# Last stage of a fused attention and expert kernel: the load queue begins a tile's rows ahead of its weight copies

## What is computed

```python
def _L1_ffn_ref(hidden_states, norm_weight, router_w, sw1, sb1, sw2, sb2, ew1, eb1, ew2, eb2):
    normed = hidden_states * rsqrt(mean(square(hidden_states)) + 1e-08) * norm_weight
    shared = jnp.maximum(normed @ sw1 + sb1, 0.0) @ sw2 + sb2
    flat = normed.reshape(-1, d)                       # 4096 tokens x 128
    probs = jax.nn.sigmoid(flat @ router_w.T)          # 8 experts
    scores, idx = jax.lax.top_k(probs, 2)
    w = scores / (jnp.sum(scores, axis=-1, keepdims=True) + 1e-06)
    comb = comb.at[jnp.arange(T)[:, None], idx].add(w)
    h = jnp.maximum(jnp.einsum('td,edh->teh', flat, ew1) + eb1, 0.0)   # hidden 512
    eo = jnp.einsum('teh,eho->teo', h, ew2) + eb2
    return shared + jnp.einsum('teo,te->to', eo, comb)
```

## Time and profile before

| What | us |
|---|---|
| median of three timed runs | 1502.99 (1501.4 to 1507.45) |
| the profiled execution's own time | 1501.84 |
| its span in the trace | 1500.0 |
| what lies around the span | 1.84 |

### The profile page before, as it was taken

How to read it: one execution, slowest core, us unless ns; L and a number is a source line. 1 busy time by engine, 2 the same in 40 slices (tenths; PEclk the granted TensorE clock), 3 DMA queues, 4 the chain that set the end, 5 groups by cost and what they waited for, 6 DMA issues and landing times. The chain is left out here.

```text
span 1500.0 us, 35809 instructions
## 1 busy us (share of the span) xinstructions
PE 1261.6 (84%) x13441; PEld 1047.8 (70%) x13441; DVE 1012.2 (67%) x2018; ACT 890.2 (59%) x1661; POOL 599.2 (40%) x650
## 2 busy tenths in 40 slices
PE   4999998399999999994899999999972576699880
PEld 3777776277877787783798889888962564587760
DVE  5888887576777677764356676767665865576662
ACT  3888887566666666653455566566642455486750
POOL 3222222155555555564223332424121575165561
PEclk9999999599999999997899999999995688799995
DMA  4222221333221332132100000000001221146646
GB/s 140 92 91 93 94 99 50 120 86 92 76 64 45 92 79 69 42 89 75 48 13 17 9 16 9 17 10 9 3 2 42 83 78 35 47 138 222 209 132 181
DMA packets 88083, 109.04 MB, mean 73 GB/s; under 512 B 13290, under 2 KB 54890, under 8 KB 87914
## 3 DMA queue, kind: packets, MB, share of 16 engines
q1 hardware_dynamic: 82922, 96.46, 20.9%
q0 software_dynamic: 4992, 10.30, 2.1%
HBM read 61.11 MB, written 29.82 MB: 61 GB/s over the span
## 5 line engine op out<-in xcount | busy, mean ns | idle before, releaser
L818 POOL TENSOR_TENSOR b_h_lo<-b_h,b_h_hi 128x512 fp32r<-128x512 f32 x168 | 216.6, 1294 | 179.7 <-ACT b_h_hi L842 179.3
L837 ACT ACTIVATE b_zg<-b_zg 128x512 f32<-128x512 f32 x168 | 97.7, 582 | 82.5 <-PE b_zg L882 82.3
L842 ACT ACTIVATE b_h_hi<-b_h 128x512 fp32r<-128x512 f32 x168 | 105.3, 627 | 64.9 <-DVE b_h L1047 64.9
L1047 DVE TENSOR_TENSOR b_h<-b_zg,b_uw 128x512 f32<-128x512 f32 x168 | 116.2, 692 | 32.1 <-ACT b_zg L837 26.8
L1919 POOL DMA_INDIRECT planes_dram<-d_y_out,d_back x92 | 94.2, 1024 | 95.3 <-DVE d_y_out L2227 68.9
L2196 DVE TENSOR_TENSOR d_h_lo<-d_h,d_h_hi 128x512 fp32r<-128x512 f32 x124 | 85.1, 690 | 66.6 <-ACT d_h_hi L1957 32.3
L1040 DVE TENSOR_TENSOR b_uw<-b_zu,b_gw 128x512 f32<-128x512 f32 x128 | 88.2, 689 | 58.0 <-PE b_zu L882 51.3
L1586 DVE TENSOR_TENSOR c_oT_lo<-c_oy,c_oT_hi 128x512 fp32r<-128x512 f32 x64 | 44.1, 689 | 93.7 <-ACT c_oT_hi L1329 93.7
L1246 POOL TENSOR_TENSOR c_prob<-c_prob,c_recip 128x512 f32<-128x512 f32 x64 | 65.5, 1045 | 99.5 <-DVE c_recip L1579 99.5
L318 POOL TENSOR_TENSOR a_qx<-a_qT,headmask 128x256 f32<-128x256 f32 x64 | 37.9, 614 | 150.5 <-ACT a_qT L353 150.5
L525 DVE TENSOR_REDUCE a_top<-a_score_ps 128x8 f32<-128x1024 f32 x64 | 78.1, 1220 | 18.7 <-PE a_score_ps L416 18.7
(11 more groups left out here) (352 smaller groups left out, 4135.4 us busy)
## 6 DMA issues: line engine op xcount, KB each, us to landing
rows_dram<-a_blank SPq DMA_DIRECT2D x32, 520.0 KB, 3.2
b_gw<-gates_dram SPq DMA_DIRECT2D x64, 256.0 KB, 3.7
d_up_slot<-d_up_tab SPq DMA_DIRECT2D x15, 512.0 KB
d_down_slot<-d_down_tab SPq DMA_DIRECT2D x15, 512.0 KB
d_xg<-rows_dram SPq DMA_DIRECT2D x23, 260.0 KB
b_gm<-gates_dram SPq DMA_DIRECT2D x32, 160.0 KB, 3.8
c_craw<-in_c_ctxT_dram SPq DMA_DIRECT2D x16, 256.0 KB, 3.0
d_pay<-planes_dram SPq DMA_DIRECT2D x16, 256.0 KB, 4.6
```

The lines of the kernel that those rows point to most:

```text
L818: pool.tensor_tensor(h_lo[:, m % HS, :], h[:, m % HF, :], h_hi[:, m % HS, :].bitcast(F32), ALU.subtract).then_inc(lo_done.sem, 1)
L837: act.activation(zg_ps[:, n % ZG, :], zg_ps[:, n % ZG, :], ACT.Silu).then_inc(sg_done.sem, 1)
L842: act.activation(h_hi[:, m % HS, :], h[:, m % HF, :], ACT.Copy).then_inc(hi_done.sem, 1)
L1047: dve.tensor_tensor(h[:, n % HF, :], zg_ps[:, n % ZG, :], uw[:, n % 2, :], ALU.mult).then_inc(h_done.sem, 1)
```

## The change

In the turn of step k the block that gathers the rows of job k+2 is moved from behind the up and down weight copies to ahead of them. For the first planned tile the rows now also wait for the plan (`planned`), since the wait that covered them stood in the weight block. Nothing is computed otherwise; number, size and queue of all transfers stay.

```diff
@@ -1839,6 +1839,22 @@
                 weights.sync(sp, *share(k, c))
                 if c:
                     return
+                if FIRST <= k + 2 < JOBS:
+
+                    t = k + 2 - FIRST
+                    if t == 0:
+                        wait_scattered(sp, GROUPS)
+                    sp.wait_ge(xT_done.sem, xT_done.at(k + 1))
+                    sp.wait_ge(tail_done.sem, tail_done.at(t - 1))
+                    if t < E:
+                        block_rows = rows[t * REGION:t * REGION + TILE, :]
+                    else:
+                        if t == E:
+                            sp.wait_ge(planned, 2)
+                        r = sp.value_load(tile_row[0:1, t - E:t - E + 1], min_val=0, max_val=E * REGION)
+                        block_rows = rows[bass.ds(r, TILE), :]
+                    sp.dma_start(xg[:, t % 2, :, :], block_rows.rearrange("(u p) f -> p u f", p=P)
+                                 ).then_inc(xg_in[t % 2], 16)
                 if MOVED <= k + 2 < JOBS:
 
                     i, slot = k + 2 - MOVED, (k + 2 - MOVED) % WS
@@ -1859,20 +1875,6 @@
                     sp.wait_ge(y_done.sem, y_done.at(k + 1 - WS + 1))
                     sp.dma_start(down_slot[:, slot, :].bitcast(F32), down_tab[:, bass.ds(e, 1), :].rearrange("p a f -> p (a f)").bitcast(F32)
                                  ).then_inc(down_in[slot], 16)
-                if FIRST <= k + 2 < JOBS:
-
-                    t = k + 2 - FIRST
-                    ...
-                    sp.dma_start(xg[:, t % 2, :, :], block_rows.rearrange("(u p) f -> p u f", p=P)
-                                 ).then_inc(xg_in[t % 2], 16)
 
             ticks(step)
```

## The result

Over 20 runs of each kernel on the same chip, the kernel after took a median of 1501.27 us (1494.04 to 1508.83) and the kernel before 1506.86 us (1499.38 to 1516.66). The ratio is **0.996, 95% interval 0.9944 to 0.9977**: the change saves 0.4%, some 6 us, where 10.2 were forecast. The profiled execution of the kernel after took 1502.43 us, its span 1500.6 us, and that is not less than the span of the profiled execution before, 1500.0 us. So the trace of after shows an execution in which nothing was won, and its question is what took the gain back.

The account below looks back on a forecast made before the run. The prediction took TensorE's 6.48 us a tile as the floor and late rows as most of the 12.8 us lost above it. Less 2.65 us that stay, 10.2 us were to go, giving 1492.8 us, range 1488.5 to 1501.5.

Parts of the forecast that it names:

- What bounds it: Planned tiles: TensorE's own work is the floor at 6.48 us a tile; 12.8 us are lost between tiles 5 and 19.
- Rows moved ahead: SyncE's queue: rows go out 4.2 to 5.8 us sooner, after the tail, and the `d_t` waits for `xg` go whole.
- Copies moved behind, at no cost: Bias, up and down go out behind the rows, bias 0.4 to 1.6 us later; 4.6 us of cover, cost nothing.
- SP's turn: SyncE's turn of loads and issues takes 5.83 us, 0.65 under the new pace; at worst 6.23.
- The rival in which SyncE sets the pace: SyncE's turn of 7.2 us leaves no gain, 1503 us (0.12, with anything unseen); longer turns make it slower, about 1510 (0.06).
- The new wait for the plan: First planned tile's rows: the added wait is on one semaphore long reached and costs nothing.
- What stays: ScalarE's late waits for `z` of TensorE, cause unknown, go on costing TensorE two gaps, 2.65 us.
- The sum: 12.8 - 2.65 = 10.2 us gained over the planned tiles, for a median of 1492.8 us.
- ScalarE's late results set the pace: Rival: late results every second tile keep 9.7 of the 12.8 us; gain 3.1, 1499.9 us; chance 0.20.

Follow-up runs that it names:

- before again: The kernel before, unchanged, run against itself in a comparison where it took about 1484 us: 1482.72 against 1483.78 us, ratio 0.9999.
- before, static: The kernel before, old order, with rows' places and experts from constants, against the kernel before: 1482.8 against 1484.2 us (0.999), 1491.04 against 1500.16 us (0.9936).
- after, third time: The kernel after, unchanged, against the kernel before in a comparison where that took 1483.78 us: 1481.0 us, ratio 0.9982.
- type S: The comparisons in which the kernel before took 1500 to 1507 us; in two others it took 1484 us.
- early loads: The kernel after with all 30 register loads made before the planned tiles' copies, against the kernel before: ratios 0.9975 twice (before near 1484 us), 0.9936 and 0.994 (1500.16, 1504.31).

## Why the prediction was right in direction and wrong in size

**What bounds it: right.** The pace of 6.48 us a tile is TensorE's own and the floor. Kernels with nothing else in the way took 123.06 to 123.08 us for 19 tiles; the prediction had 123.16.

**Rows moved ahead: right.** They were to go out 1.2 to 2.4 us after the tail. In after a tail's last step ends at 1362.22 + 0.16 = 1362.38 and the rows go out at 1364.10, 1.7 us later. The waits of `d_t` for the DMA of `xg` are gone, in every profile of the new order.

```profile
1362.22 0.16 DVE L2240 SCALAR_TENSOR_TENSOR d_back<-d_pad,d_tail 128x4 int32<-128x4 f32 x1
```

**Copies moved behind, at no cost: right.** No view of after names a wait for `up_slot` or `down_slot`, not even where SyncE's turn took 6.49 us from rows to down: the 4.6 us of cover held. From the rows' issue to the bias an undisturbed turn needs 0.89 us (1409.87 to 1410.76); the prediction took 1.48.

**SP's turn: right**, for undisturbed turns. 1409.87 to 1416.42 is 6.55 us, the pace of the tiles, and TensorE never waits for it. One reading in it was wrong: that no turn of before without a wait exceeds 6.2 us. From the rows at 1394.27 to those at 1400.86 are 6.59 us, and `y_sb` (1395.13) and the tail that SyncE asked for (1394.12) had long ended; it is one of the turns with slow steps. The rival in which SyncE sets the pace is out: TensorE's waits name neither slot's DMA, and tiles come at 6.48 us wherever there is no hold.

**The new wait for the plan: right**, nothing of it is seen.

**What stays: the step that failed.** The prediction gave 2.65 us to ScalarE's late results and the other 10.2 of the 12.8 us to the late rows. It is the other way about. The late rows by themselves cost 3.3 us (before again), 3.1 and 2.1 us (before, static). The remaining 9.6 us or more of before came with the holds and were absent where there were none; what stayed in after was 14.4, 7.3 and 7.0 us, not 2.65. That most of it was disguised in before is argued from the traces and not shown by itself: the holds of before stand beside slow steps of SyncE, up to 0.70 us for a register step that took 0.18 at most in before again, and behind slow steps what came last was the rows. Even in the table only 6.6 us of TensorE's waits named the rows; the other 3.6 of the 10.2, the restarts too short to be listed, were given to them without a reason. The table of waits put the time down to `xg`, since it names the last comer, and the prediction read that as the cause. In the earlier trace rows ScalarE's waits for `z` have 21.2 us. Some 10 us of that is ordinary and costs nothing (after, third time, has 10.0 in 16 waits of up to 0.6 us and loses none), but the rest is in long waits, and the earlier trace rows showed two of them behind matmuls that had long finished; the prediction wrote that down, said that it couldn't tell the cause, and priced only the two gaps of TensorE that they ended last.

It also took for granted that what stays stays as it was. On type S the one profile of before has four holds of 2.46 to 4.54 us, the three of after have one or two of 4.8 to 6.7 us. One of those outlasts the slack between jobs, leaves TensorE idle for 4.4 to 4.8 us at a stretch, and brings down the granted clock, which the small gaps never did (0.97 to 0.96 in place of 1.00). Why they differ in shape was not shown.

**The sum.** The medians of type S gained 5.6 us in the first comparison and 3.1 and 3.5 in the two later ones. The loss was 12.9 us in one profile of before, and 14.4, 7.3 and 7.0 in three of after, 9.6 in the mean: 3.3 less. That agrees, though with one profile of before it could hardly fail to be near. Between one and two holds an execution lie 7 us, so a single pair of profiles could not have shown a gain of this size, and the pair above showed none. The low end of the range has a slip of 0.1 us: 1490.2 less 1.6 is 1488.6.

**The rivals.** The first, "ScalarE's late results set the pace", was the nearest in its mechanism and its time (1499.9 forecast, 1501.27 measured), though it expected one gap of 1.39 us in every second tile and not one or two long ones. Its gain of 3.1 us is what the two later comparisons gave. Its support, that such waits come in the stretch with copies and not before, holds against 1300 to 1332 us only: around 1240 us they were longer. At 0.20 its chance was too low: the wait with the largest sum at ScalarE had no explanation, and an unexplained wait ought to have held more of the chance than the 2.65 us gave it. The measured time lies within the range, 0.2 us from its upper end. That says little: the range was built on a median of 1502.99 us from three executions, and the twenty of the comparison have 1506.86. By the bound of 0.5% the result is no change.

## What to carry to other kernels

A wait's releaser is the one that came last, not the cause: before the sum of such a line is taken as what a change wins, look whether the engine named, and the queue that feeds it, are themselves slow in those turns and quick in others; if they are, find out by what. A wait for an engine whose records show it as long finished is time of its own and doesn't go when the next best cause is removed; price it with all that is long beyond the ordinary wait of the same operation in an undisturbed stretch, not only with the part that happens to end last. Where addresses for DMAs come out of registers beside heavy traffic, reading the registers in a quieter stretch cost nothing here, and in the one comparison with holds that had both kernels side by side the median was 0.3 to 0.4% lower, which is likely but not clear of the spread. And where a cause comes and goes between comparisons, run before and after in the same one and look at both traces before explaining a difference.

## What the runs showed of the hardware

- News of finished matmuls can be kept back by microseconds. ScalarE waited 4.8 to 6.7 us for a result where the pace of a whole tile is 6.48, and seven updates of TensorE then came within 0.32 us, in each of the four long holds of the kernel after. SyncE was slow in the same moments: its turn from rows to down took 6.49 us in one of them, 3.74 and 3.84 us in two others, against 2.84 undisturbed. In the planned tiles it was seen with copies and register-addressed issues together, and in none of the six profiles of the slower kind from which the copies, the rows' register work or the experts' was taken away. Earlier in the execution, around 1240 us, it came without copies too.
- Bytes alone didn't do it in the planned tiles: 216 to 223 GB/s with static addresses, in full or in part, left TensorE busy for 105.00 of 105 us.
- It isn't there in every comparison. The same kernel before took 1484 us in two of the comparisons and 1500 to 1507 in the others; the new order gained on both, 3.1 to 5.6 us and 2.8. Behind 1100 us the profiles of the slower kind hold 3181 to 3879 records of semaphore updates, the others 5768 to 6040.
- Gaps of 3.0 to 4.8 us in TensorE's work (six, four of them in after and two in early loads) each came with 3.4 to 6.8 us at the 1.2 GHz level, begun in the gap or right behind it, while gaps of up to 1.4 us left the clock at 1.00.
